# First experts' blocks: inner values formed transposed, gate and up weights copied by ScalarE to fixed places, register loads without bounds

## The reference, cut to what matters

```python
def _L2_ffn_ref(hidden_states, w_router, gate_up_proj, down_proj, w_gate, w_up, w_down):
    x = hidden_states.reshape(-1, h)
    logits = x @ w_router.T
    _, top_idx = jax.lax.top_k(logits, TOP_K)
    mask = jax.nn.one_hot(top_idx, E, dtype=logits.dtype).sum(axis=1)
    scores = jax.nn.sigmoid(logits) * mask
    masked_inputs = scores.T[:, :, None] * x[None, :, :]
    gate_up = jnp.einsum('eth,ehf->etf', masked_inputs, gate_up_proj)
    gate, up = jnp.split(gate_up, 2, axis=-1)
    expert_out = jnp.einsum('etf,efh->eth', up * jax.nn.silu(gate), down_proj)
    shared = jax.nn.silu(x @ w_gate.T) * (x @ w_up.T) @ w_down.T
    out = shared + expert_out.sum(axis=0)
```

## Time and profile before

| what | value |
|---|---|
| runs without the profiler, median (lowest to highest) | 900.95 us (893.62 to 903.18), 3 runs |
| span of the profiled execution, first to last instruction | 904.6 us |
| busy in the span: TensorE matmuls, VectorE, ScalarE, GpSimd | 87%, 63%, 51%, 45% |
| share of the chain that ended last: TensorE, VectorE, GpSimd | 62%, 18%, 7% |
| block loop of the first experts, first transpose to last scatter issued | 585.2 to 637.4 us |

### The profile page before, as it was taken

One profiled execution on the slowest core, in us unless ns is written; L12 is line 12 of the kernel. 1 busy time (PEld: TensorE's weight loads), 2 busy tenths in 40 slices (PEclk: granted clock), 3 DMA queues, 4 the chain that ended last, 5 costly groups with the idle time before them and its releaser, 6 DMA issues.

```text
span 904.6 us, 21435 instructions
## 1 busy us (share of the span) xinstructions
PE 785.5 (87%) x8139; PEld 563.6 (62%) x8139; DVE 572.4 (63%) x1514; ACT 464.0 (51%) x1088; POOL 405.1 (45%) x556
## 2 busy tenths in 40 slices
PE   6997977899989979999779987399579997899996
PEld 2675744767867767876357765155456775566665
DVE  5647869898798656886689783223488895211212
ACT  2215647588787636766248663044167573333331
POOL 3129736677566432443268750335666673000101
PEclk9558888799999997999859995689699997799998
DMA  8017000000000000000090000300155700000000
GB/s 315 2 39 218 3 1 1 1 1 2 2 2 1 2 1 2 3 3 3 2 279 3 3 3 1 91 25 35 45 187 164 212 3 3 1 1 0 4 9 13
DMA packets 35571, 38.02 MB, mean 42 GB/s; under 512 B 8736, under 2 KB 26528, under 8 KB 34960
## 3 DMA queue, kind: packets, MB, share of 16 engines
q1 hardware_dynamic: 34480, 34.61, 12.8%
q0 software_dynamic: 992, 2.04, 0.6%
HBM read 28.37 MB, written 8.27 MB: 41 GB/s over the span
## 4 chain that ended last, share of the span: by engine, by line
PE 62%; DVE 18%; POOL 7%; issue 6%; ACT 4%; DMA 2%; SPq 0%; DVEq 0%; POOLq 0%; ACTq 0%
PE bank L1003 7%; PE bank L1013 6%; PE bank L783 6%; PE bank L804 5%; PE bank L792 4%; PE bank L963 3%; PE bank L701 3%; PE bank L819 3%; PE bank L873 2%; DVE pairs L1525 2%; PE bank L694 2%; POOL rstd L1763 2%; PE bank L850 2%; DVE pairs L1521 2%; PE bank L759 1%
## 5 line engine op out<-in xcount | busy, mean ns | idle before, releaser
L1762 POOL TENSOR_SCALAR veps<-mv 128x1 f32<-128x1 f32 x112 | 27.0, 241 | 238.2 <-DVE mv L1410 238.0
L1791 POOL TENSOR_TENSOR sm<-sm,mx 128x512 f32<-128x512 f32 x80 | 83.9, 1052 | 43.5 <-DVE mx L1475 42.9
L1118 ACT COPY pT<-bank 128x512 f32<-128x512 f32 x112 | 65.5, 585 | 41.2 <-PE bank L792 39.8
L1113 ACT ACTIVATE pr<-sm 128x512 f32<-128x512 f32 x112 | 70.2, 632 | 24.0 <-POOL sm L1791 23.2
L792 PE MATMUL bank<-W,pr 128*128 128x128 f32 x448 | 73.7, 289 | 7.7 <-ACT pT L1118 6.3
L1786 POOL TENSOR_TENSOR pairs<-KS,quad 128x512 f32<-128x512 f32 x56 | 60.1, 1075 | 39.1 <-ACT KS L1095 39.1
L1696 DVE SCALAR_TENSOR_TENSOR XB_id<-bank,QM,XB_id 128x128 f32<-128x128 f32 x64 | 18.0, 345 | 93.8 <-PE bank L1013 93.8
L783 PE MATMUL bank<-pairs,Q 64*128 64x256 f32 x448 | 71.0, 439 | 2.3 <-DVE sm L1472 0.9
L1763 POOL TENSOR_TENSOR rstd<-veps,W 128x1 f32<-128x1 f32 x112 | 65.2, 582 | 9.3
L1003 PE MATMUL bank<-XT,big 128*128 128x512 f32 x128 | 66.0, 644 | 2.5 <-ACT G L1260 2.5
L804 PEld LDWEIGHTS bank<-VX,pT 64*64 64x64 f32 x3584 | 60.2, 139 | 12.3 <-issue 6.6
(11 more groups left out here) (303 smaller groups left out, 1933.8 us busy)
## 6 DMA issues: line engine op xcount, KB each, us to landing
big<-gup SPq DMA_DIRECT2D x4, 1024.0 KB, 9.4
rel_scratch<-G SPq DMA_DIRECT2D x16, 256.0 KB, 2.8
W<-small SPq DMA_DIRECT2D x1, 3206.5 KB, 12.0
big<-early SPq DMA_DIRECT2D x2, 1557.0 KB, 8.5
big<-down SPq DMA_DIRECT2D x8, 256.0 KB, 8.9
QM<-rel_scratch SPq DMA_DIRECT2D x16, 128.0 KB, 2.8
PM<-rel_scratch SPq DMA_DIRECT2D x16, 128.0 KB, 2.7
big<-e3w SPq DMA_DIRECT2D x2, 1024.0 KB, 7.6
```

The costliest lines, as they stand in the source:

```text
L1113: act.activation(pr[:, u % 2, 4 * h:4 * h + 4, :, :].rearrange("p g b k -> p b g k"), sm[:, 2 * (u % 2) + h, :].rearrange("p (b g k) -> p ...
L1118: act.copy(pT[:, u % 2, 4 * h:4 * h + 4, :], bank[BK[f"tu{h}"]][:, :].rearrange("p (h n) -> p h n", h=4)).then_inc(pt_ready, 1)
L1791: tt(v, v, bc(mx[:, slot, :], [P, 8, S], 2), ALU.subtract).then_inc(pcentered, 1)
```

## The change

TensorE's `up` now holds the expert's weights stationary, in four tiles of 128 by 128, and moves the block `XE` past them, so that the 256 gate and 256 up values come out with the inner index on the partitions and the tokens on the columns. This is what `down_` needs as its stationary operand, so `turn` and `turned_out` are gone. The stationary tiles are read from a fixed place: ScalarE copies the 512 columns of the block's expert, addressed by a register of its own, to one of four places (`fetch`, in `staged_w`), three blocks ahead. For that ScalarE loads the 23 offsets too, 8 between `gates(0)` and `gates(1)` and 15 after. The copy of the transposed block goes from ScalarE to VectorE. All register loads are without bounds.

```diff
                 def up(j):
                     pe.wait_ge(xe_ready, j + 1)
-                    mm(fill(2 + j % 2, mid_ready)[:, :], XE[j % 4], big[:, bass.ds(start[j], 2 * NF2)], start=True,
-                       stop=True).then_inc(gate_mid, 1)
-
-                def turn(j):
+                    pe.wait_ge(staged, j + 1)
+                    ps = fill(2 + j % 2, mid_ready)
+                    for c in range(4):
+                        last = mm(tile(ps, c), tile(staged_w[j % 4], c), XE[j % 4], start=True, stop=True)
+                    last.then_inc(gate_mid, 1)
+
+                def down_(j):
                     pe.wait_ge(mid_ready, 4 + j + 1)
-                    ps = fill(4 + j % 2, hT_ready)
-                    for c in range(2):
-                        last = pe.transpose(ps[:, c * P:(c + 1) * P], HB[j % 4][:, c * P:(c + 1) * P], ident)
-                    last.then_inc(h_turned, 1)
-
-                def down_(j):
-                    pe.wait_ge(hT_ready, j + 1)
                     ps = fill(6 + j % 2, block_ready)
                     for c in range(2):
-                        last = mm(ps[:, 0:P], HBT[j % 4][:, c * P:(c + 1) * P],
+                        last = mm(ps[:, 0:P], tile(HB[j % 4], c),
                                   big[:, 2 * NF2 + c * P:][:, bass.ds(start[j], P)], start=(c == 0), stop=(c == 1))
                     last.then_inc(block_full, 1)
...
-                start = [pe.value_load(owner[0:1, j:j + 1], min_val=0, max_val=(NE2 - 1) * WIDE2) for j in range(BLOCKS)]
-                for i in range(BLOCKS + 4):
-                    for lag, work in ((4, down_), (3, turn), (1, up), (0, take)):
+                start = [pe.value_load(owner[0:1, j:j + 1]) for j in range(BLOCKS)]
+                for i in range(BLOCKS + 3):
+                    for lag, work in ((3, down_), (1, up), (0, take)):
                         if 0 <= i - lag < BLOCKS:
                             work(i - lag)
...
-                def copied(j):
+                def fetch(j):
                     if j >= 4:
                         act.wait_ge(gate_mid, 4 + j - 3)
-                    act.wait_ge(xe_full, j + 1)
-                    act.copy(XE[j % 4], bank[j % 2][:, 0:P]).then_inc(xe_ready, 1)
+                    act.copy(staged_w[j % 4], big[:, bass.ds(start[j], 2 * NF2)]).then_inc(staged, 1)
 
                 def gated(j):
                     if j >= 4:
-                        act.wait_ge(h_turned, j - 3)
+                        act.wait_ge(block_full, j - 3)
                     act.wait_ge(gate_mid, 4 + j + 1)
                     act.activation(HB[j % 4], bank[2 + j % 2][:, 0:NF2], ACT.Silu).then_inc(silu_ready, 1)
...
                 gates(0)
+                act.wait_ge(slot_ready, 2)
+                start = [act.value_load(owner[0:1, j:j + 1]) for j in range(8)]
                 gates(1)
-                for i in range(BLOCKS + 3):
-                    for lag, work in ((3, turned_out), (1, gated), (0, copied)):
-                        if 0 <= i - lag < BLOCKS:
-                            work(i - lag)
+                start += [act.value_load(owner[0:1, j:j + 1]) for j in range(8, BLOCKS)]
+                act.wait_ge(e2_in, 16 * 14)
+                for j in range(3):
+                    fetch(j)
+                for j in range(BLOCKS):
+                    gated(j)
+                    if j + 3 < BLOCKS:
+                        fetch(j + 3)
...
+                def copied(j):
+                    if j >= 4:
+                        dve.wait_ge(gate_mid, 4 + j - 3)
+                    dve.wait_ge(xe_full, j + 1)
+                    dve.tensor_copy(XE[j % 4], bank[j % 2][:, 0:P]).then_inc(xe_ready, 1)
+
...
                 for i in range(BLOCKS + 3):
-                    if i >= 3:
-                        result(i - 3)
-                    if i < BLOCKS:
-                        hidden(i)
+                    for lag, work in ((0, copied), (1, hidden), (3, result)):
+                        if 0 <= i - lag < BLOCKS:
+                            work(i - lag)
```

More of the change, by code:

```diff
@@ L445, in decoder @@
         HB = [sm[:, 2 + i // 2, (i % 2) * NF2:(i % 2 + 1) * NF2] for i in range(4)]
-        HBT = [G[:, i // 2, (i % 2) * NF2:(i % 2 + 1) * NF2] for i in range(4)]
         YB = [pT[:, i // 8, i % 8, :] for i in range(16)] + [G[:, 2 + i // 4, (i % 4) * P:(i % 4 + 1) * P]
@@ L472, in decoder @@
         QTp = room(7168, 256, "p (j n) -> p j n", j=2)
+        staged_w = [cap[:, i // 2].rearrange("p b k -> p (b k)")[:, (i % 2) * 2 * NF2:(i % 2 + 1) * 2 * NF2] for i in range(4)]
         e2_w = room(0, NE2 * WIDE2, "p (e n) -> p e n", e=NE2)
@@ L523, in decoder @@
         q_product, k_product = (sem(n) for n in ("q_product", "k_product"))
[L526 to L529, removed]
+        logit_full, choice_full, rank_full, gate_mid, up_mid, xe_full, block_full = (sem(n) for n in (
+            "logit_full", "choice_full", "rank_full", "gate_mid", "up_mid", "xe_full", "block_full"))
+        score_ready, choice_ready, silu_ready, xe_ready, staged, xs_ready = (sem(n) for n in (
+            "score_ready", "choice_ready", "silu_ready", "xe_ready", "staged", "xs_ready"))
         lg_ready, one_ready, slot_ready, mid_ready, block_ready = (sem(n) for n in (
```

## The result

Over 20 runs each, the changed kernel has a median of 894.62 us (884.49 to 903.14) and the kernel before one of 898.51 (893.56 to 909.02). The ratio is 0.9935, with a 95% interval of 0.9909 to 0.9960: faster by 5.8 us, somewhere between 3.6 and 8.2. The ratio leaves out the slow runs of both kernels, so it isn't the ratio of the two medians. The forecast was 8.0 us off the median of three runs known then (900.95), 893.0, with a range of 888.5 to 899.

A forecast was written before the change was run, and what follows sets the result against it. The loop was taken as bound by the dependences up, silu, copied, up (1.90 us a round), the entry by register loads. Gains 3.5 + 4.3 + 0.2 = 8.0 us off 900.95 gave 893.0 us, range 888.5 to 899.

The forecast's parts named there:

- Entry: Before the block loop: TensorE's loads without bounds end before the blocks land, so the first transpose starts 3.0 us earlier.
- ScalarE's loads: ScalarE's 23 register loads before the loop: 0.49 us each, costing nothing up to 0.57 each.
- the good bound: ScalarE's register loads before the loop: at most 0.57 us each costs nothing; 0.6 was the bad side.
- The rival of slow loads: At the entry: register loads cost 0.6 us each, the entry gains 1.6 less, 894.6 us; chance 0.12.
- The copy of the weights: In the loop: ScalarE's weight copy takes 0.63 us, 1.15 us of ScalarE work per block, hidden under the round.
- The rival in which ScalarE sets the round: In the loop: ScalarE's copy by register takes 1.5 us, the round stays at 1.89, 897.3 us; chance 0.12.
- The loop at full clock: Settled block rounds at 2.4 GHz: each falls from 1.89 to 1.65 us, 18 rounds bringing 4.3 us.
- The ring: In the loop: the dependences take, copied, up, take set the new round, summing to 1.66 us, taken as 1.65.
- The clock: Start of the loop: full clock comes 9.7 us after the first transpose, as before, giving 3.5 us gain by up(4).
- The fourth rival: In the loop: full clock never comes as TensorE stops for copied every round; 2.77 us rounds, 913 us; chance 0.05.
- The tail: End of the loop: last scatter issued 5.0 us behind the last up instead of 5.2, gaining only 0.2.
- The rival of TensorE alone: In the loop: TensorE's own work sets the round at 1.45 us, 11.6 us gained, 889.3 us; chance 0.13.

The follow-up runs named there:

- the repeat: Changed kernel with no edit, profiled and timed again beside the kernel before; stage 60.6 us, ratio 0.9917 to the kernel before.
- bounds_both: Changed kernel with bounds put back on all 46 register loads, TensorE's and ScalarE's; stage from owner to last scatter 62.7 us, round 1.72 us.
- before_no_check: Kernel before, TensorE's register loads given compiler-known bounds with no check at load or use; stage 64.5 us, round 1.89, ratio 0.9935.
- lead2: Changed kernel with no bounds checks anywhere and blocks taken one round earlier; stage 55.0 us, round 1.51, ratio 0.9847 to the kernel before.
- copied_on_act: Changed kernel with the copy of the transposed block put back on ScalarE, behind the silu; stage 61.9 us, round 1.86 us.
- no_check: Changed kernel with compiler-known bounds and the check left out everywhere, on both engines; stage 59.4 us, round 1.72, ratio 0.9905 to the kernel before.
- unbounded_only: Kernel before with only the bounds taken off TensorE's register loads; stage 71.5 us, round 2.18 us.
- before_lead2: Kernel before with no checks on TensorE's register values and blocks taken one round earlier; stage 57.2 us, round 1.635, ratio 0.9885.

## Why the prediction was right, point by point

**The stage.** The sum was 8.0 us, the stage gained 8.2 (7.1 in the repeat). Whole time: 5.8 and 7.5, by ratio. I had put a gain below 1% as the likelier case, and it is one.

**Entry: right.** 3.0 was predicted; the first `take` comes 16.7 us after `owner` before and 13.6 after, 3.1 earlier, and T in `bounds_both` and `before_no_check` gives 3.2. TensorE's loads end well before the landing. VectorE's first product behind `gates(1)` was pushed back 0.8 us, and nobody waited for it.

**ScalarE's loads: right, in the direction of the good bound.** I took 0.49 and 0.57 as the limit. They start (566.7 - 564.3) / 7 = 0.34 us apart, and the first `fetch` starts at 573.7, 4.6 us before it is needed. The rival of slow loads is out. The Trainium skill ("DMA: Bandwidth & Descriptors", section on latency and other measured facts) gives about 600 ns as the floor of a `tensor_load`; the measured medians here are 303 ns on TensorE and 280 on ScalarE, and the measurement decides.

**The copy of the weights: right.** 0.63 was taken, it is 0.618 and nobody waits for `staged`. The rival in which ScalarE sets the round is out.

**The loop at full clock: the mechanism right, the term mis-sized.** The ring was named, and three experiments show it (`lead2`, `copied_on_act`, `no_check`). Its sum was put at 1.65 and measured 1.72: 0.38 + 0.29 + 0.06 + 0.99. The largest piece of the 0.07 is the last, 0.03: from the start of `up` to the next `take` I used 0.96, taken from an `up` of the kernel before with its two weight loads. The other three pieces were 0.01 short each, and the sum of 1.66 was rounded down by 0.01. Over 18 rounds the loop took 31.2 us where 29.7 were forecast, 1.5 too many; 0.3 of it is the difference of the mean round, 1.735, from the 1.72 of the kernel without checks.

**What I did not see: where the checks go.** The part on the entry costed the missing bounds at a gain and nothing else. They come back at each use, 0.29 us for each block in the place where it was measured (`unbounded_only`). In this kernel they cost nearly nothing, only because the ring is as long as TensorE's work with them; in the kernel before they cost more than the entry gains. That the forecast did not suffer from it is luck. The own work of the kernel before, too, was put a little too high: 1.68, where `before_lead2` runs a round in 1.635.

**The clock: the other error, and it made up for the first.** I let full clock come 9.7 us after the first transpose, "as now". It was really 10.0 in the kernel before, and in the changed one 6.1. The profiles rule out two reasons. It isn't the earlier entry: `bounds_both`, with the entry of the kernel before, has 6.5, and `before_no_check`, with that of the changed one, has 9.3. And it doesn't take the transposed form: `before_lead2` is without it and has 6.5. What sets it stays open. Up to up(4) the forecast had a gain of 3.5 us; measured from `owner`, up(4) starts at 596.87 - 568.48 = 28.4 before and 587.15 - 563.85 = 23.3 after, 5.1 earlier. From there to up(22) it was 4.3, and 630.95 - 596.87 = 34.1 became 618.33 - 587.15 = 31.2, 2.9. With the tail's 0.2 the sums are 3.5 + 4.3 + 0.2 = 8.0 and 5.1 + 2.9 + 0.2 = 8.2: two errors of about 1.5 us cancelled. The fourth rival (the clock stays low because TensorE stops in every round) is out: full clock held to the end of the loop in every profile (0.99 or 1.00), with rounds of 1.51 to 2.18. The seven extra rounds after which it was to decide are one too few by its own numbers: (2.77 - 1.65) x 7 = 7.8, less than 8.0.

**The tail: right.** +5.0 forecast, 5.0 measured, with GpSimd's three scatters 1.26 apart.

**The rival of TensorE alone** (11.6 us, a round of 1.45) is what `lead2` gives when the ring is opened: T lower by 12.7 than before. It was rightly put as less likely for this change.

## What to carry to other kernels

When an engine is recorded as busy all through a loop, compare the distance of the starts with the sum of its own work: here 1.90 against 1.68 as counted and 1.635 as measured later, and the difference named the ring of dependences that sets the round. Try first to open such a ring by the order of the work (here one block more in flight, two edited lists and loops, took 7.3 us off the stage, 64.5 to 57.2, and the new form of the computation 5.0). And a bounds check that is taken off a register load may come back at every use of the value: look for it in the sequencer's rows, not only at the load.

## What the runs showed of the hardware

- A check at the use of a register value (arithmetic of up to 0.165 us and an assertion of 0.018) between a wait and a matmul made TensorE start 0.29 us later, more than the two durations. At the loads it was alike: without the check they follow each other 0.27 us sooner (0.66 to 0.39), and the two durations are 0.146 and 0.018. Bounds that are stated to the compiler with the check left out avoid it in both places (`before_no_check`: round 1.89, T lower by 3.2).
- Full clock came 10.0, 9.4 and 9.3 us after the first transpose in the three profiles with the order of the kernel before, and 6.1 to 6.5 in the nine others. TensorE was recorded busy for 9.02 of the 10.03 us in the kernel before, for 5.35 of 6.12 in the changed one and for 6.23 of 6.45 in `before_lead2`. What makes the difference isn't shown.
- The register load took 280 ns on ScalarE and 303 on TensorE, and without bounds the loads follow each other at 0.34 and 0.39 us.
- The part of the kernel ahead of `owner`, which no edit touches, took between 558.95 and 568.48 us in the twelve profiled executions: 9.5 us, more than the change is worth. TensorE's mean granted clock over it was 0.87 in the longest, and 0.89 in the six shortest. Only a stretch that begins and ends in the changed layer could tell the kernels apart.
